# First tile of a fused cross-attention and feed-forward kernel: GpSimd's casts and looks each wait for a named VectorE result, K's bias is split in halves, and half of the second V projection goes ahead of the transposes

## The reference

```python
def xattn(src, tgt, mask, ...):          # src: context 128x512, tgt: layernorm(x) 128x256
    k, v = split(src @ W_src.T + b_src)  # each 128x256, rows times mask
    q = (tgt @ W_tgt.T + b_tgt) * mask
    scores = q_h @ k_h.T / sqrt(32)      # 8 heads of 32, masked keys at -inf
    upd = softmax(scores) @ v_h
    return concat(tgt, upd) @ W_out.T + b_out
def ffn(x):                              # w1, w2: 256->1024, h1, h2: 1024->1024, w3: 1024->256, entries -1, 0, 1
    h = silu(x @ w1.T * w1_s) * (x @ w2.T * w2_s)
    h = gelu(h @ h1.T * h1_s)
    h = gelu(h @ h2.T * h2_s)
    return h @ w3.T * w3_s
x = x + xattn(ctx, layernorm(x), mask, mask, ...)
x = x + ffn(layernorm(x))
```

## Time and profile before

| what | us |
|---|---|
| median of 3 executions | 917.93 (917.21 to 917.94) |
| the profiled execution | 916.03 |
| its span, first to last instruction | 914.2 |
| TensorE busy in the span | 904.5 (99%) |
| VectorE, ScalarE, GpSimd busy | 616.0, 389.7, 77.8 |
| granted TensorE clock, mean | 1.000 |

### The profile page before, as it was taken

The page is one execution under the profiler, slowest core; times in us unless marked ns, Lnnn a source line. Parts: engine busy times, 40 slices in busy tenths (PEclk is TensorE's granted clock), DMA queues, the critical chain, the costliest instruction groups (busy, mean ns, idle before and its releaser), DMA issues.

```text
span 914.2 us, 20846 instructions
## 1 busy us (share of the span) xinstructions
PE 904.5 (99%) x7600; PEld 863.5 (94%) x7600; DVE 616.0 (67%) x1224; ACT 389.7 (43%) x1098; POOL 77.8 (9%) x102
## 2 busy tenths in 40 slices
PE   8899999999999999999999999999999999999998
PEld 7789999999999999999999999999999999999998
DVE  6886758578585775758767576675857858576453
ACT  6782523525344353533526235252352534465231
POOL 3634001010000100001000010100101000000000
PEclk9999999999999999999999999999999999999999
DMA  9922132411324123142221423114241132303000
GB/s 354 372 85 74 35 122 70 120 41 58 91 69 120 49 74 85 51 120 57 98 62 41 121 69 117 38 34 121 69 120 42 60 87 69 92 23 105 24 13 14
DMA packets 82348, 79.20 MB, mean 87 GB/s; under 512 B 8592, under 2 KB 74896, under 8 KB 82320
## 3 DMA queue, kind: packets, MB, share of 16 engines
q1 hardware_dynamic: 81744, 78.31, 27.7%
q10 hardware_dynamic: 576, 0.52, 0.2%
HBM read 51.55 MB, written 27.26 MB: 86 GB/s over the span
## 4 chain that ended last, share of the span: by engine, by line
PE 95%; DVE 3%; issue 1%; DMA 0%; POOL 0%; ACT 0%; SPq 0%; DVEq 0%; ACTq 0%
PE F L627 58%; PE G L627 7%; PE F L738 7%; PE G L620 6%; PE G L514 5%; PE G L478 5%; PE G L496 2%; PE S L531 2%; PE G L603 2%; PE S L467 0%; DMA cT<-ctx_t 0%; DVE g L1235 0%; DVE mx L1113 0%; DVE pr L1106 0%; DVE pr L1081 0%
## 5 line engine op out<-in xcount | busy, mean ns | idle before, releaser
L627 PE MATMUL F<-hBh,H 128*128 128x256 f32 x1008 | 239.7, 283 | 0.1
L853 ACT ACTIVATE g<-F,firsts 128x256 f32<-128x256 f32 x250 | 104.6, 471 | 315.9 <-PE F L627 315.7
L627 PE MATMUL F<-hBl,H 128*128 128x256 f32 x1008 | 236.7, 279 | 0.0
L627 PE MATMUL F<-hAh,H 128*128 128x256 f32 x992 | 234.8, 281 | 0.1
L627 PE MATMUL F<-hAl,H 128*128 128x256 f32 x992 | 233.1, 279 | 0.0
L627 PEld LDWEIGHTS F<-hBh,H 128*128 128x128 f32 x1008 | 189.6, 188 | 0.6 <-ACT g L853 0.3
L627 PEld LDWEIGHTS F<-hBl,H 128*128 128x128 f32 x1008 | 189.4, 188 | 0.4
L627 PEld LDWEIGHTS F<-hAh,H 128*128 128x128 f32 x992 | 186.3, 188 | 2.2 <-ACT sil L846 0.4
L627 PEld LDWEIGHTS F<-hAl,H 128*128 128x128 f32 x992 | 186.5, 188 | 0.0
L1254 DVE CAST hBh<-g 128x512 fp32r<-128x512 f32 x64 | 27.9, 436 | 138.6 <-ACT g L853 138.6
L881 ACT ACTIVATE pr<-pr,nmx 128x128 f32<-128x128 f32 x240 | 92.7, 389 | 1.1 <-DVE nmx L1089 0.9
(11 more groups left out here) (161 smaller groups left out, 1505.7 us busy)
## 6 DMA issues: line engine op xcount, KB each, us to landing
p_dram<-pb SPq DMA_DIRECT2D x30, 512.0 KB, 3.3
pr<-p_dram SPq DMA_DIRECT2D x120, 128.0 KB, 3.2
H_raw<-h SPq DMA_DIRECT2D x16, 512.0 KB, 13.8
cT<-ctx_t SPq DMA_DIRECT2D x14, 512.0 KB, 3.3
x_dram<-xt SPq DMA_DIRECT2D x28, 256.0 KB, 2.3
out<-y SPq DMA_DIRECT2D x32, 128.0 KB, 1.7
x_in<-x_t SPq DMA_DIRECT2D x15, 256.0 KB, 2.7
x2T<-x_dram SPq DMA_DIRECT2D x60, 64.0 KB, 1.9
```

Source lines behind the costliest of these rows:

```text
L627: return mm(bank, W[0][:, k, cols], part[:, k, :], start=first, stop=last)
L853: fn(g[:, q % 2, m, :], mid_bank(f, q)[:, m, :], ACT.Gelu, scale=scols[:, col:col + 1]).then_inc(gelu_ready, 1)
```

## The change

Nothing is computed differently. One look (chunk 3) goes from GpSimd to ScalarE. Each of GpSimd's remaining casts and looks in tile 0's attention gets a wait on a result of VectorE (`mask_bias_ready`, `xn_ready`, `xn2_ready`, `h_ready`). ScalarE's looks are dealt out anew between its other work. On VectorE `bias_mask_k(1)` is cut into its two instructions, and these go behind the statistics of the two halves of tile 0; `ln2_apply_0(1)` goes ahead of `x2_lo_0(0)`; and in tile 0's feed-forward part `bias_mask_k(2)` goes ahead of split 3 and of the masking of tile 1's second half of scores. On TensorE `project_v(1, [0])` goes ahead of `transpose_p_0(0, ...)`.

```diff
@@ -268,7 +268,7 @@
         chunks = [(src[:, k:k + CH // W.shape[2], :], raw[:, k:k + CH // W.shape[2], :], W[:, k:k + CH // W.shape[2], :])
                   for src, raw, W in big for k in range(0, W.shape[1], CH // W.shape[2])]
         assert len(chunks) == CHUNKS
-        on_pool = [3, 9, 12]
+        on_pool = [9, 12]
         on_act = [n for n in range(CHUNKS) if n not in on_pool]
 
         def wait_x(engine, a):
@@ -772,8 +772,8 @@
 
             def first_attention():
 
+                project_v(1, [0])
                 transpose_p_0(0, (0, 1))
-                project_v(1, [0])
                 out_proj_x_0(0)
                 transpose_p_0(1, (0,))
                 attend_0(0)
@@ -947,10 +947,10 @@
                 for q in range(4):
                     silu(f, q)
                     if first:
-                        look((on_act[10:11], on_act[11:13], [], [])[q])
+                        look((on_act[10:12], on_act[12:13], on_act[13:14], on_act[14:15])[q])
                 if first:
                     copy_xnT(2)
-                    look(on_act[13:])
+                    look(on_act[15:])
                 if a is not None:
                     if not early:
                         exps(a, 0)
@@ -981,18 +981,19 @@
             exps_0(1)
             look(on_act[3:4])
             copy_pT_0(0)
+            look(on_act[4:5])
             copy_upd_0(0)
             copy_pT_0(1)
-            look(on_act[4:6])
+            look(on_act[5:6])
             copy_upd_0(1)
+            copy_xnT(1)
             look(on_act[6:7])
-            copy_xnT(1)
             keep_xnT(1)
+            look(on_act[7:8])
             act.wait_ge(firsts_loaded, 16)
             x2_hi_0(0)
-            look(on_act[7:9])
             x2_hi_0(1)
-            look(on_act[9:10])
+            look(on_act[8:10])
             tile(0, 1, 2)
             with act.Fori(1, TILES - 3) as i:
                 tile(i, i + 1, i + 2)
@@ -1036,12 +1037,12 @@
                 wait_mrow(dve, a)
                 V.tensor_scalar(mbias[:], mrow_of(a), 0.0, MASKED, ALU.is_equal, ALU.mult).then_inc(mask_bias_ready, 1)
 
-            def bias_mask_k(a):
+            def bias_mask_k(a, cs=range(KD)):
 
                 wait_mrow(dve, a)
                 dve.wait_ge(scores_done, at("scores_done", a - 1, 1))
                 dve.wait_ge(k_done, at("k_done", a, 2))
-                for c in range(KD):
+                for c in cs:
                     V.scalar_tensor_tensor(kT[:, c, :], k_part(a, c), bcols[:, c:c + 1],
                                            mrow_of(a), ALU.add, ALU.mult).then_inc(kT_ready, 1)
 
@@ -1293,14 +1294,15 @@
                 if first:
                     row_max(1, 0)
                 gate_times_up(f, 3)
+                split(f, 2)
+                if first:
+                    bias_mask_k(n)
+                split(f, 3)
                 if first:
                     mask_scores(1, 1)
-                split(f, 2)
-                split(f, 3)
-                if n is not None:
+                    row_max(1, 1)
+                elif n is not None:
                     bias_mask_k(n)
-                if first:
-                    row_max(1, 1)
                 if n is not None:
                     mask_bias(n)
                     bias_mask_q(n)
@@ -1369,18 +1371,19 @@
             normalise_0(0)
             copy_pT_0(0)
             normalise_0(1)
-            bias_mask_k(1)
             mask_bias(1)
             ln1_stats(1)
             copy_pT_0(1)
             ln1_apply(1)
             residual_ln2_stats_0(0)
             count_low_bits(0, EARLY)
+            bias_mask_k(1, [0])
             ln2_apply_0(0)
             residual_ln2_stats_0(1)
+            bias_mask_k(1, [1])
             raise_flag(0)
+            ln2_apply_0(1)
             x2_lo_0(0)
-            ln2_apply_0(1)
             bias_v(1)
             x2_lo_0(1)
             ln1_stats(2)
@@ -1459,24 +1462,27 @@
             for n in range(EARLY - 1):
                 cast(n)
             add_bias(0)
-            pool.wait_ge(kT_ready, at("kT_ready", 1, 1))
-            look(on_pool[0])
+            pool.wait_ge(mask_bias_ready, at("mask_bias_ready", 1, 1))
             cast(EARLY - 1)
             inverse_std1(1)
+            pool.wait_ge(xn_ready, at("xn_ready", 1, 2))
             cast(EARLY)
             inverse_std2_0(0)
+            pool.wait_ge(xn2_ready, at("xn2_ready", 0, 1))
             sum_low_bits(0)
             cast(EARLY + 1)
             inverse_std2_0(1)
-            for n in range(EARLY + 2, EARLY + 4):
-                cast(n)
-            look(on_pool[1])
+            pool.wait_ge(xn2_ready, at("xn2_ready", 0, 2))
+            look(on_pool[0])
+            cast(EARLY + 2)
             inverse_std1(2)
             pool.wait_ge(h_ready, at("h_ready", 0, 1))
-            look(on_pool[2])
+            cast(EARLY + 3)
+            pool.wait_ge(xn_ready, at("xn_ready", 2, 2))
+            cast(EARLY + 4)
             pool.wait_ge(h_ready, at("h_ready", 0, 2))
-            for n in range(EARLY + 4, EARLY + 6):
-                cast(n)
+            look(on_pool[1])
+            cast(EARLY + 5)
             pool.wait_ge(h_ready, at("h_ready", 0, 4))
             for n in range(EARLY + 6, EARLY + KH):
                 cast(n)
```

## The result

| | before | after |
|---|---|---|
| median, first measurement (6 executions each) | 917.76 us | 914.04 us |
| ratio, its 95% interval | | 0.9957 (0.9948 to 0.9967) |
| ratio in a second measurement (5 executions) | | 0.9952 (0.9939 to 0.9966) |
| the profiled execution, its span | 916.03, 914.2 us | 913.24, 911.5 us |

The ratio 0.9957 is 3.9 us of 917.8; the medians differ by 3.7. 4.2 us (0.46%) had been forecast. The interval lies clear of 1.

What follows compares the result with a forecast made beforehand. VectorE's chain to x2_ready, standing for GpSimd, was taken to set when TensorE's unbroken work starts. 3.81 + 0.82 - 0.09 - 0.1 = 4.4, less 0.2 behind x2_ready, gives 4.2 us: 913.7 us, range 912.8 to 916.0.

Steps and rivals of the forecast that it cites:

- The losses that go: VectorE up to x2_ready: mask bias 1.44, tile 1's normalisation pair 0.70, two x2 normalisations 1.67 stop standing for GpSimd; 3.81 us.
- K's bias: VectorE, tile 1: its 0.87 us leaves the chain for pauses behind the statistics, about 0.05 comes back; 0.82 gained.
- V's place: TensorE, V's first half ahead of the transposes: costs nothing up to 0.1; TensorE's work up to the residual about 1 us earlier.
- The swap of `x2_lo_0(0)` and `ln2_apply_0(1)`: VectorE before x2_ready: the first now comes behind the second, 0.42 less a 0.33 us wait for ScalarE; 0.09 lost.
- Behind x2_ready: From x2_ready to tile 1's attention: two more ScalarE looks and new collisions; 0 to 0.6 us lost, 0.2 taken.
- Cast 9: GpSimd's cast collides with VectorE's scaling of the maxima behind x2_ready; 0 to 0.8 us.
- The second flag: Ahead of the middle layers: its lead shrinks from 2 us to under 1 us; its path can cost up to 0.5.
- The 0.77 ahead of V: TensorE's wait ahead of V of tile 2: goes because `bias_mask_k(2)` comes earlier; nothing of the 0.77 us remains as gain.
- The read of probabilities: Tile 1's attention: exponentials come 0.66 us later, slack of 0.6 is used up, second half not before +36.5 from x2_ready.
- Rival A: Later stretch takes back more (cast 9, second flag, read of probabilities): gain 2.0 to 3.4, 914.5 to 915.9 us; chance 0.2.
- Rivals B and C: B: no change, 916.1 to 918 us, chance 0.07. C: slower, GpSimd's chain bounds feed-forward, 919 to 920, chance 0.03.
- The page's rule: VectorE's two-port instructions and GpSimd's exclude each other throughout; moved look and cast 9 could cost 0.3, making the sum 3.9.

Runs made afterwards that it cites:

- run 2: The changed kernel without GpSimd's five new waits (mask_bias_ready, xn_ready, xn2_ready); ratio to the kernel before 0.9999 (0.9989 to 1.0009).
- run 7: The changed kernel with cast 9 waiting for the scaled maxima and cast 6 behind the power of tile 2; 912.12 us in one execution, beside 918.03 before.
- run 4: The changed kernel with K's bias of tile 1 in one piece at its old place, ahead of the mask bias; ratio to the kernel before 0.9966.
- run 3: The changed kernel with the first half of tile 1's V behind the transposes again; ratio to the kernel before 0.9961 (0.9948 to 0.9973).
- run 1: The kernel before with GpSimd's new list alone (named waits, chunk 3's look on ScalarE); ratio to the kernel before 0.9986 (0.9976 to 0.9995).
- run 5: The kernel before with GpSimd's new list and ScalarE's new dealing of looks; 916.19 us in one execution, beside 918.03 for the kernel before.
- run 8: The changed kernel with one look moved from ahead of ScalarE's first silu to behind it; 913.05 us in one execution, beside 918.03 before.
- the changed kernel again: The changed kernel unaltered, timed a second time; ratio to the kernel before 0.9952 (0.9939 to 0.9966).
- run 11: The changed kernel with VectorE's list of tile 0's feed-forward part as before (K's bias of tile 2 behind split 3); 913.85 us in one execution.
- run 9: The changed kernel with early look count, casts 6 and 9 clear of VectorE's scalars, one look behind the first silu; ratio to before 0.9944.
- run 10: The kernel of run 9 with chunk 10's look on GpSimd, waiting for res_ready, ahead of cast 6; ratio to the kernel before 0.9961 (0.9947 to 0.9974).

## Why the prediction was right, point by point

**The losses that go.** Forecast 1.44 + 0.70 + 1.67 = 3.81 us; measured 1.44 + 0.69 + 1.67 = 3.80. That the lengths are GpSimd's is shown by run 2, where three come back with the casts, and by run 7 for two others. For the mask bias it rests on its look alone, which lies beside it before and is gone after; no run brings it back. The 0.1 put down for the one-column variance beside cast 5 was not lost: it took 0.15.

**K's bias and V's place.** Forecast 0.82 and about 0. K's bias gave 0.77, and about 0.1 came back at the two powers; run 4 confirms it with 0.71. V's place is the term that was mis-sized in this stretch. Its cost had been put at up to 0.1, because the copy of the transposes was thought to come late enough; it is 0 to 0.45, and 0.36 in the profiled execution. Its use, TensorE about 1 us earlier, had no term in the sum, and run 3 gives it 1.08. The margin of 0.3 us for every output of TensorE was too wide: VectorE waits 0.28 for the transposes, and the output projection of half 1 ends at 29.52, 0.2 ahead of the instruction that takes it (29.73). The swap of `x2_lo_0(0)` and `ln2_apply_0(1)` came out at nothing (0.09 lost was forecast), though in runs 1 and 5, without it, VectorE stood nearly 1 us there and the normalisation came 0.7 late.

So 3.8 + 0.8 - 0.1 - 0.4 = 4.1: X came 4.14 us earlier, 4.4 forecast. The steps can't be told apart by adding: run 1 gives 2.1 and run 2 gives 1.3, both with the moved look, and all together 4.14, because in run 1 the lists of TensorE and ScalarE take over, and in run 2 the casts are back.

**Behind x2_ready.** Forecast 0.2 lost, in bounds of 0 to 0.6; lost 0.58 at the attention. This is the term that was mis-sized most, and it had three parts. Silu 0 came at X + 2.94, as worked out (2.9). Cast 9 made the scaling 1.0 longer, above its bound of 0.8, though taking that away moved middle by only 0.11 (run 7). The second flag had been given up to 0.5, with a lead of under 1 us: the flag is written at 54.11 and middle's first product starts at 55.05, and this 0.94 returned in runs 2, 3, 4, 7 and 8 and in the changed kernel again; so it was the last thing waited for, and middle came at + 21.46 where +20.5 to +21.0 had been given, 0.04 short of the +21.5 that was to prove the prediction wrong. K's projection starts at +10.44, 0.61 later than before (9.83), where 0.3 to 0.5 had been given. The 0.77 ahead of V went as said, and run 11 shows that the move was worth more than the 0.77: without it the wait grows to 1.73.

**The read of probabilities.** Forecast as what holds the second half of the attention at X + 36.5. Run 9 finds that wall at +36.34, but in the changed kernel it was not the bound: middle was later still. So the loss had the size of the forecast's upper bound by another wait than the one that I had put first, and that the number fits is luck. The short wait at the attention, named as a sign, did not appear. Rival A named these parts with more weight; the changed kernel's loss stayed short of it. Rivals B and C did not come: no cast held a power back in the changed kernel (0.19 us is the longest wait of that kind for x2), though run 4 shows how near it is (0.63 against 0.58). H1's casts were done at 51.97, ahead of middle at 55.05.

**The page's rule.** By the rule of the Trainium skill (SBUF — State Buffer, "SBUF: two separate sides") the moved look would hold VectorE to its end. In the changed kernel the only instruction of a held kind beside a look is the scaling at 45.04, which cast 9 holds anyway, so the 0.3 of the rule had no occasion. The scaling ended at 46.21 and cast 9 at 46.18, as an exclusive hold would have it within 0.2; the look beside the cast of run 10 ended VectorE's wait at about 37.8 (38.20 less the free 0.43), an estimate that is 0.4 ahead of the look's recorded end at 38.22, as in the earlier trace rows. The rule's two-input case, of which no row before told, shows in run 10: 1.42 where 0.69 is free.

**The total.** 4.14 - 0.44 (what the gate of tile 1 shows behind X) = 3.70 us up to tile 1, 3.9 by the ratio, 4.2 forecast. The mechanism was right; the first stretch gave 0.3 less than forecast, the second lost 0.2 more up to the gate.

## What to carry to other kernels

An instruction whose length in one place is a multiple of its length elsewhere may be waiting: look at what GpSimd does at that moment, and place that work behind a named result, in front of instructions that it does not hold (here statistics and those that read PSUM). Before adding up what several mends give, ask which list is the bound once the first is made. When a distance between two marks scatters, look for the one instruction ahead of which it scatters, and measure from there: 0.45 us of scatter became 0.03. Small instructions, of eight or two columns, are held until the cast is through, like big ones (1.17 and 0.65 us, where 0.17 is free).

## What had not been expected of the hardware

The hold goes both ways. In run 9 cast 6, from 35.88, took 1.30 us instead of 1.03, beside VectorE's copy of the residual. A variance instruction with one column ran free (0.15 us at 30.98) beside a cast from 30.17 to 31.20, while one with two columns (0.65) and a scaling of eight (1.17) stood; why one column is free, no run here settles. And TensorE's next product starts 0.94 us after VectorE has written the flag, in the seven traces in which the flag comes last (changed twice, runs 2, 3, 4, 7 and 8).
